# Sorting pass of a two-layer graph kernel: GpSimd is paced by later TensorE groups, and in the middle of each group too

## The chip, the cores and the metric

One Trainium2 chip, and one core of it. The metric is the device time of one execution in microseconds (us), the median over several.

## The reference, cut to what matters

Two graph layers over 6250 nodes and 206250 edges. For this change only the first matters, and of it the part before the sum over the edges of a source node:

```python
h = jnp.maximum(_layernorm(x, axis=-1), 0.0)
att_scores = jax.nn.sigmoid(head_rel @ att_w + att_b)      # head = h[src], rel by edge type
neighbor_emb = att_scores * tail                           # tail = h[dst], 64 wide
aggr_emb = jax.ops.segment_sum(neighbor_emb, edge_index[0], num_segments=N_ENTITIES)
```

The second layer sums over the same source nodes (`segment_sum(msg_j, row, ...)`). The edges come ordered by `dst`, and both sums go by `src`. So the kernel first sorts the edges by `src`: it writes one record per edge to HBM at the place that it has in the order of `src`. A record is `REC` = 100 numbers: the edge's 32 attributes, its two nodes, its gate, a pad, and its 64 gated values.

## The kernel before

The kernel runs as one stage after another: `front`, `sort` (the sorting pass, 220 to 2870 us of the trace), `relation_layer`, `relation_nodes`, and the second layer. The change lies in `sort` alone.

**Tiles, groups, chunks.** `P` = 128 edges, one per partition, are a tile. `G` = 4 tiles are a group. A chunk is `T` = 26 tiles, so `GROUPS` = 7 groups, of which the last has two tiles. There are `CHUNKS` = 62 chunks, 434 groups. A loop turn (`Fori` over `i`) has two chunks, `n = 2*i` and `2*i + 1`, with double buffers `b`. The turns `i = 0` and `i = 30` are written out, the others are a loop.

**Engines.** Every engine has its own program, and semaphores that count groups tie them together. A program is worked through in its order.

- TensorE, per group q: three "rows" matmuls (3 partitions by 512 columns) that spread the low digit, the source and the destination of each edge over all partitions: `p_lo` (L666), `p_src` (L668), `p_dst` (L670). `p_dst` raises `s_dst`. Then `p_place` (L674), four matmuls. Then `look` for the group before, q-1: twelve matmuls `p_look` (L643), the last of which raises `s_look`, and twelve matmuls `p_h` (L653), which raise `s_h`. These 28 load 128x128 weights each. `p_src` of a group waits for VectorE's ranks of the group before (`s_ranked`).
- VectorE, per group q: `table_rest` (L847), `dst_hot` (L850, waits for `s_dst` of q and `s_h` of q-2), `table_low` (L852), `same_before` (L860, four of them, ends with `s_ranked`), then `picked` of group q-1 (L807, waits for its `s_look`), the one-hot tiles of the next chunk (L511, L512), a sum (L815) and `logit` (L820). `place` (L826) comes once a chunk, after its last group.
- ScalarE, per group: `table` (L708), `lo_away` (L711), `lo_hot_t` (L714), the gate (L724), `h_gated` (L730). Once a chunk it assembles the records in `rec[b]` and raises `s_ready`.
- SyncE: per chunk the loads `fields`, `window`, `stage`, and a write of zeros to `q_starts`.
- GpSimd: 26 indirect DMAs per chunk (L625, "scatters"), one per tile, that write `rec[b][:, t, :]` to `records` at `place[b][:, t]`.

**What paces GpSimd.** A chunk's scatters may begin when its places and records are there (`s_place`, `s_ready`; ScalarE has them in group 2 of the chunk after). From `i = 1` on, GpSimd also waits for `s_dst` at t = 4, 8, 12, 16, 20, 24: at tile t of chunk n, until `p_dst` has been done for `7*n + LEAD + t/4` groups in all, with `LEAD` = 12. `rows_spread` gives this number. In the written-out last turn (chunks 60 and 61) it is cut off at 434. Tiles t = 0 to 3 have no such wait, so the scatters t = 24, 25 and 0 to 3 of the next chunk go under one wait. After each wait GpSimd raises a semaphore `s_passed`, which nothing waits for.

**Buffers.** `rec[b]` and `place[b]` are written again for chunk n+2, when all 26 scatters of chunk n have landed (`s_sent[b]`).

Of the kernel before, what the change touches and what calls it, by code (L numbers as in the profile page):

```python
# [36 lines left out]
G = 4  # L37
# [23 lines left out]
LO, NODE, TO = 0, 1, 2  # L61
H3 = 2 * D + D // 2
STEP_A, STEP_B, STEP_C, STEP_D = 7, 10, 13, 23
LEAD = 12
COLS = -(-NT // P)
LAST_COLS = NT - (COLS - 1) * P

# [32 lines left out]
def loop(eng, body):  # L100


    body(0)
    with eng.Fori(1, PAIRS - 1) as i:
        body(i)
    body(PAIRS - 1)
# [45 lines left out]
def at_start(i, b=0):  # L152
    return isinstance(i, int) and i == 0 and b == 0
# [361 lines left out]
def sort(k):  # L515
# [5 lines left out]
    with ExitStack() as ctx:  # L521
# [49 lines left out]
        def rows_spread(n, g):  # L571

            ahead = n * GROUPS + LEAD + g
            return min(ahead, CHUNKS * GROUPS) if isinstance(n, int) else ahead
# [9 lines left out]
        with nc.Block() as block:  # L584
            @block.sync
            def _(sp):
                sp.wait_ge(s_set, 2)

                def body(i):
                    for b in range(2):  # L590
                        n = 2 * i + b
                        wait(sp, s_dst, (n - 1) * GROUPS)
                        sp.dma_start(fields[b][:], k.field_rows[:, bass.ds(n * P * T, P * T)]).then_inc(s_fields[b], 16)
                        base = sp.value_load(k.base_i[0:1, bass.ds(n, 1)], min_val=0, max_val=ROWS - P)
                        wait(sp, s_h, (n - 1) * GROUPS)
                        sp.dma_start(window[b][:], k.h3_table[bass.ds(base, P), :]).then_inc(s_window[b], 16)
                        if not at_end(i, b):
                            wait(sp, s_staged, n - 1)
                            sp.dma_start(stage[b][:], attr_v[bass.ds(n, 1), :, :, :].rearrange("c p t e -> (c p) t e")).then_inc(s_attr[b], 16)

                        sp.dma_start(q_starts_v[:, bass.ds(n * T, T), :], zero_q[:].rearrange("p (t c) -> p t c", c=QW)).then_inc(s_zq, 16)

                loop(sp, body)
                sp.wait_ge(s_zq, 16 * CHUNKS)
                for b in range(2):
                    sp.wait_ge(s_sent[b], SCATTERED * PAIRS)

            @block.gpsimd
            def _(pool):
                def body(i):  # L610
                    for b in range(2):
                        n = 2 * i + b
                        if not at_start(i, b):
                            pool.wait_ge(s_place, n + GROUPS)
                            pool.wait_ge(s_ready, n + GROUPS)
                            pool.sem_inc(k.s_passed, 1)
                        for t in range(T):
                            if at_start(i, b) and t % G == 0:
                                pool.wait_ge(s_place, t // G + 1)
                                pool.wait_ge(s_ready, t // G + 1)  # L620
                                pool.sem_inc(k.s_passed, 1)
                            elif not (isinstance(i, int) and i == 0) and t > 0 and t % G == 0:
                                pool.wait_ge(s_dst, rows_spread(n, t // G))
                                pool.sem_inc(k.s_passed, 1)
                            nc.gpsimd.indirect_dma_start(  # L625
                                k.records, bass.IndirectOffsetOnAxis(ap=place[b][:, t:t + 1], axis=0),
                                rec[b][:, t, :], None).then_inc(s_sent[b], 16)

                loop(pool, body)
# [1361 lines left out]
```

## Time and profile before

| | |
|---|---|
| median of 3 runs | 5864.14 us (5855.48 to 5867.09) |
| the profiled execution's own time | 5865.56 us |
| its span, first to last instruction | 5863.7 us |
| sorting pass, from the first scatter to the last | 233.4 to 2866.3 us |
| mean granted TensorE clock over the span | 0.531 |

The span is what the trace covers, and 1.9 us lie around it. Engines in the rows: PE is TensorE, PEld its weight loads, DVE VectorE, ACT ScalarE, POOL GpSimd, SPq SyncE's DMA queue. A row of the timeline is the start, the duration, the engine, the line, the operation and its tiles, and in brackets how long the engine had been idle before it and what released it. "remote" and "issue" as releasers mean that the profile could not put the end of the wait down to a recorded instruction. Ends of matmuls are modelled: a PE row says when a matmul was issued, not when its result was there. When it was there is seen in the engine that waited for it.

### The profile page before, as it was taken

How to read it: one execution, taken by the hardware profiler on the slowest of the kernel's cores; microseconds unless marked ns; L12 is line 12 of the kernel's file. 1: busy time of each engine (PE TensorE's matmuls, PEld its weight loads, DVE VectorE, ACT ScalarE, POOL GpSimd, SP SyncE). 2: the span in 40 equal slices, each digit the busy share in tenths (PEclk: the TensorE clock that was granted, in tenths of full speed). 3: DMA queues.
4: the chain of work that ended last, by engine and by line, in shares of the span. 5: the costliest groups of instructions: out<-in, count | busy, mean ns of one | idle time of the engine just before them, and what ended most of it. 6: DMA issues, size and time to landing. Idle time of an engine off the chain costs nothing. (4 is left out here: it accounts for less than half of the span.)

```text
span 5863.7 us, 79660 instructions
## 1 busy us (share of the span) xinstructions
PE 2726.4 (46%) x21110; PEld 1693.1 (29%) x21111; DVE 3881.4 (66%) x8751; ACT 2758.0 (47%) x5413; POOL 3278.9 (56%) x3388
## 2 busy tenths in 40 slices
PE   7655555555555555555488622322223222222223
PEld 7433333333333333333388511111111111111102
DVE  9867777777777777776599645655556666655552
ACT  3244444444444444444122345655555555555552
POOL 0146565666666565656610266666666666666653
PEclk8555555555555555555577755555555555555555
DMA  5112121212121212121477533433334343433321
GB/s 64 55 54 71 63 71 62 71 63 71 63 71 63 71 63 71 63 71 58 103 160 145 72 103 100 124 110 108 108 103 111 109 110 103 110 108 109 109 79 24
DMA packets 691304, 505.28 MB, mean 86 GB/s; under 512 B 588446, under 2 KB 605214, under 8 KB 691109
## 3 DMA queue, kind: packets, MB, share of 16 engines
q1 hardware_dynamic: 573012, 246.99, 18.2%
q0 software_dynamic: 108736, 196.93, 11.6%
q10 hardware_dynamic: 9360, 59.56, 2.7%
q14 instruction: 172, 1.40, 0.1%
q8 instruction: 24, 0.39, 0.0%
HBM read 289.96 MB, written 213.26 MB: 86 GB/s over the span
## 5 line engine op out<-in xcount | busy, mean ns | idle before, releaser
L625 POOL DMA_INDIRECT records<-rec,place x1612 | 1557.2, 966 | 1306.9 <-issue 451.0
L1395 POOL DMA_INDIRECT got_a<-kv_table,idx_a x1612 | 1539.5, 955 | 762.8 <-issue 691.9
L860 DVE SCALAR_TENSOR_TENSOR same_before<-p_src,src_f,before 128x128 bf16<-128x128 f32 x1612 | 775.0, 535 | 0.0
L711 ACT ACTIVATE lo_away<-p_lo,minus_number 128x512 bf16<-128x512 f32 x434 | 291.2, 671 | 615.5 <-remote 593.6
L668 PE MATMUL p_src<-fields,select 3*128 3x512 bf16 x434 | 248.3, 572 | 687.7 <-DVE same_before L860 512.0
L1411 PE MATMUL p_a<-ident,flat_attr 128*128 128x128 f32 x434 | 123.5, 433 | 930.5 <-issue 447.4
L807 DVE TENSOR_TENSOR picked<-p_look,hi_hot 128x392 f32<-128x392 f32 x434 | 231.5, 533 | 407.5 <-remote 398.2
L1420 PE MATMUL p_a<-relu,w_t 128*128 128x512 f32 x248 | 230.8, 1034 | 463.4 <-issue 332.5
L850 DVE TENSOR_SCALAR dst_hot<-p_dst,number 128x512 bf16<-128x512 f32 x434 | 307.3, 708 | 191.1 <-remote 178.1
L643 PE MATMUL p_look<-table_low,lo_hot_t 128*128 128x98 bf16 x1612 | 410.2, 281 | 0.0
L643 PE MATMUL p_look<-table_rest,lo_hot_t 128*128 128x98 bf16 x1612 | 409.4, 280 | 0.0
L1545 DVE TENSOR_TENSOR prod<-got_a,wide 128x1664 f32<-128x1664 f32 x62 | 117.0, 1888 | 440.2 <-remote 216.3
L643 PE MATMUL p_look<-table,lo_hot_t 128*128 128x98 bf16 x1612 | 402.3, 278 | 0.0
L730 ACT ACTIVATE h_gated<-p_h,gate_s 128x64 f32<-128x64 f32 x1586 | 372.1, 315 | 51.5 <-remote 12.2
L653 PE MATMUL p_h<-window,dst_hot 128*128 128x64 bf16 x4836 | 357.6, 242 | 65.1 <-issue 64.9
L1014 PE MATMUL acc<-high,lo_r 128*128 128x64 bf16 x1708 | 345.4, 244 | 60.0 <-DVE low L1079 40.7
L708 ACT COPY table<-p_place 128x49 f32<-128x49 f32 x434 | 91.7, 211 | 597.0 <-issue 371.6
L1411 PEld LDWEIGHTS p_a<-ident,flat_attr 128*128 128x128 f32 x434 | 75.6, 215 | 978.3 <-issue 824.4
L1014 PE MATMUL acc<-rest_r,lo_r 128*128 128x64 bf16 x1708 | 344.3, 243 | 0.0
L1014 PE MATMUL acc<-low,lo_r 128*128 128x64 bf16 x1708 | 344.2, 243 | 0.0
L653 PEld LDWEIGHTS p_h<-window,dst_hot 128*128 128x128 bf16 x4836 | 312.2, 133 | 54.2 <-issue 53.8
L1014 PEld LDWEIGHTS acc<-high,lo_r 128*128 128x128 bf16 x1708 | 291.3, 171 | 67.6 <-issue 66.3
(377 smaller groups left out, 8443.3 us busy)
## 6 DMA issues: line engine op xcount, KB each, us to landing
sums<-packed_a ACTq DMA_DIRECT2D x62, 936.0 KB
q_starts<-zero_q SPq DMA_DIRECT2D x62, 884.0 KB
rec_r<-records SPq DMA_DIRECT2D x124, 442.0 KB
qin<-q_starts SPq DMA_DIRECT2D x62, 884.0 KB
attr_a<-records SPq DMA_DIRECT2D x62, 442.0 KB
records<-rec,place POOLq DMA_INDIRECT x1612
got_a<-kv_table,idx_a POOLq DMA_INDIRECT x1612
stage<-in_edge_attr SPq DMA_DIRECT2D x61, 416.0 KB
```

What stands on the lines that cost most here:

```text
L625: nc.gpsimd.indirect_dma_start(k.records, bass.IndirectOffsetOnAxis(ap=place[b][:, t:t + 1], axis=0), rec[b][:, t, :], None).then_inc(s_se ...
L643: last = nc.tensor.matmul(p_look[qb][:, j * 2 * HI:(j + 1) * 2 * HI], lo_hot_t[qb][:, j * P:(j + 1) * P], part, start=(e == 0), stop=(e == 2))
L653: last = nc.tensor.matmul(p_h[qb][:, j * D:(j + 1) * D], dst_hot[qb][:, j * P:(j + 1) * P], part, start=(e == 0), stop=(e == 2))
L668: nc.tensor.matmul(p_src[:, 0:m * P], k.select[:, NODE, :], rows, start=True, stop=True).then_inc(s_src, 1)
L711: nc.scalar.activation(lo_away[qb][:, 0:m * P], p_lo[:, 0:m * P], ACT.Abs, bias=k.minus_number[:]).then_inc(s_lo_away, 1)
L730: last = nc.scalar.activation(to, p_h[qb][:, j * D:(j + 1) * D], ACT.Copy, scale=gate[b][:, t:t + 1])
L807: v.tensor_tensor(picked[:, 0:n, :, :], p_look[gb][:, 0:n * 2 * HI].rearrange("p (g a h) -> p g a h", a=2, h=HI), bc(group_hot(k, b, g, HI ...
L850: v.tensor_scalar(dst_hot[qb][:, 0:m * P], p_dst[:, 0:m * P], k.number[:], None, ALU.is_equal).then_inc(s_dst_hot, 1)
L860: last = v.scalar_tensor_tensor(same_before[:, first:first + j + 1, :].rearrange("p g e -> p (g e)"), p_src[:, 0:(j + 1) * P], k.src_f[:, ...
L1014: last = nc.tensor.matmul(acc[:, to(t // SUPER)], lo[b][:, :, t], part, start=False, stop=True, skip_group_check=True)
L1395: nc.gpsimd.indirect_dma_start(got[b][:, t, :], None, k.kv_table, bass.IndirectOffsetOnAxis(ap=idx[b][:, t:t + 1], axis=0)).then_inc(s_got ...
L1420: nc.tensor.matmul(p_a[:, 0:c1 - c0], k.w2_t[:], relu[:, c0:c1], start=True, stop=True).then_inc(s_net, 1)
```

## The change

Two edits. `LEAD` goes from 12 to 14, so each wait at t = 4, 8, ... is for two groups more of `p_dst`. And a second kind of wait is added in the middle of each group of scatters, at t = 2, 6, 10, 14, 18, 22: until `look` has been done for `7*n + 13 + (t-2)/4` groups (`rows_spread(...) - 1`). Both hold in all turns but the first.

```diff
-LEAD = 12
+LEAD = 14
...
                             elif not (isinstance(i, int) and i == 0) and t > 0 and t % G == 0:
                                 pool.wait_ge(s_dst, rows_spread(n, t // G))
                                 pool.sem_inc(k.s_passed, 1)
+                            elif not (isinstance(i, int) and i == 0) and t % G == G // 2:
+                                pool.wait_ge(s_look, rows_spread(n, t // G) - 1)
+                                pool.sem_inc(k.s_passed, 1)
                             nc.gpsimd.indirect_dma_start(
                                 k.records, bass.IndirectOffsetOnAxis(ap=place[b][:, t:t + 1], axis=0),
                                 rec[b][:, t, :], None).then_inc(s_sent[b], 16)
```

## Rows read from the trace of the kernel before

**Rows 1.** The page: the span, and its costliest group, with its idle time.

```profile
span 5863.7 us, 79660 instructions
...
L625 POOL DMA_INDIRECT records<-rec,place x1612 | 1557.2, 966 | 1306.9 <-issue 451.0
```

**Rows 2.** Busy time by stretch: us, then each engine's busy us (x instructions), clock, DMA share.

```profile
276.80:310.50 33.70, 25.38 (x227) 14.85 (x225) 32.71 (x123) 21.07 (x64) 0.38 (x1) 0.50 0.05 16
...
321.80:348.40 26.60, 1.63 (x3) 0.23 (x3) 2.69 (x10) 2.30 (x7) 17.24 (x18) 0.50 0.11 37
...
1498.40:1539.60 41.20, 23.23 (x204) 13.62 (x203) 29.57 (x109) 19.56 (x60) 25.21 (x26) 0.50 0.23 78
...
1622.00:1664.80 42.80, 23.39 (x205) 13.48 (x203) 30.23 (x111) 19.74 (x60) 24.98 (x27) 0.50 0.18 55
```

**Rows 3.** Who waited for whom, 500 to 2500 us: in total, times, longest.

```profile
DVE picked L807 <- remote: 283.3, 95, 6.1
DVE dst_hot L850 <- remote: 135.7, 40, 4.9
DVE table_rest L847 <- issue: 72.8, 24, 3.3
...
POOL records L625 <- issue: 343.6, 1059, 2.1
POOL records L625 <- PE p_dst L670: 225.0, 107, 2.5
POOL records L625 <- remote: 222.7, 85, 3.2
```

**Rows 4.** Timeline of POOL: the scatter after each longer pause, and two others.

```profile
1505.62 0.96 POOL L625 DMA_INDIRECT records<-rec,place  x1 [2.33 <-PE p_dst L670]
1506.88 0.96 POOL L625 DMA_INDIRECT records<-rec,place  x1 [0.30 <-issue]
...
1512.25 0.96 POOL L625 DMA_INDIRECT records<-rec,place  x1 [1.88 <-PE p_dst L670]
...
1524.58 0.96 POOL L625 DMA_INDIRECT records<-rec,place  x1 [2.52 <-remote]
...
1529.77 0.96 POOL L625 DMA_INDIRECT records<-rec,place  x1 [0.30 <-issue]
...
1537.11 0.96 POOL L625 DMA_INDIRECT records<-rec,place  x1 [2.59 <-remote]
...
1546.83 0.96 POOL L625 DMA_INDIRECT records<-rec,place  x1 [2.42 <-PE p_dst L670]
```

**Rows 5.** Timeline of all engines in the run of scatters from 1524.58 us.

```profile
1523.80 0.75 DVE L850 TENSOR_SCALAR dst_hot<-p_dst,number 128x512 bf16<-128x512 f32 x1 [4.84 <-remote]
...
1526.47 0.56 DVE L807 TENSOR_TENSOR picked<-p_look,hi_hot 128x392 f32<-128x392 f32 x1
...
1527.01 0.63 PE L670 MATMUL p_dst<-fields,select 3*128 3x512 bf16 x1
...
1528.43 0.74 DVE L850 TENSOR_SCALAR dst_hot<-p_dst,number 128x512 bf16<-128x512 f32 x1
...
1528.64 0.28 PE L643 MATMUL p_look<-table_low,lo_hot_t 128*128 128x98 bf16 x1
...
1534.65 0.57 DVE L807 TENSOR_TENSOR picked<-p_look,hi_hot 128x392 f32<-128x392 f32 x1 [3.47 <-remote]
```

**Rows 6.** Timeline: VectorE's wait at the end of the next run, of six scatters.

```profile
1545.82 0.57 DVE L807 TENSOR_TENSOR picked<-p_look,hi_hot 128x392 f32<-128x392 f32 x1 [1.83 <-remote]
```

**Rows 7.** Timeline of DVE and POOL: before chunk 1's scatters, and around them.

```profile
281.28 0.74 DVE L850 TENSOR_SCALAR dst_hot<-p_dst,number 128x512 bf16<-128x512 f32 x1
...
311.63 0.96 POOL L625 DMA_INDIRECT records<-rec,place  x1 [34.45 <-ACTq L762]
...
343.25 0.96 POOL L625 DMA_INDIRECT records<-rec,place  x1 [0.30 <-issue]
...
348.40 0.57 DVE L807 TENSOR_TENSOR picked<-p_look,hi_hot 128x392 f32<-128x392 f32 x1 [23.92 <-remote]
```

**Rows 8.** Timeline of DVE, POOL and ACT at the end of the pass.

```profile
2799.39 0.96 POOL L625 DMA_INDIRECT records<-rec,place  x1 [6.74 <-PE p_dst L670]
...
2802.86 0.48 DVE L850 TENSOR_SCALAR dst_hot<-p_dst,number 128x256 bf16<-128x256 f32 x1
...
2825.07 0.36 DVE L807 TENSOR_TENSOR picked<-p_look,hi_hot 128x196 f32<-128x196 f32 x1 [14.94 <-remote]
...
2830.75 0.52 ACT L730 ACTIVATE h_gated<-p_h,gate_s 128x64 f32<-128x64 f32 x2 [4.49 <-remote]
...
2834.66 0.96 POOL L625 DMA_INDIRECT records<-rec,place  x1 [7.43 <-issue]
...
2866.31 0.96 POOL L625 DMA_INDIRECT records<-rec,place  x1 [0.30 <-issue]
...
2871.83 5.99 SPq L964 DMA_DIRECT2D rec_r<-records  x4
```

## The prediction, made before the change was run

> **What bounds the kernel now.** I read the page first, then the busy time by stretch, the waits, and last the timeline, because the pass repeats itself from chunk to chunk and one turn tells nearly all.
>
> The page says that the scatters are the costliest group of the kernel, 1612 of 0.966 us, and that GpSimd stands idle before them for 1306.9 us in all [rows 1]. So GpSimd isn't simply full. By stretch, a chunk takes 41.20 us, and one in four takes 42.80, 1.6 more. VectorE is busy for 29.57 to 30.23 us of that, GpSimd for 25.21, TensorE for 23.23 by its modelled rows, ScalarE for 19.56, and the DMA engines to 23% [rows 2]. No engine is full. The mean chunk is (3 x 41.20 + 42.80) / 4 = 41.6 us.
>
> While GpSimd had nothing to do (276.8 to 310.5 us) VectorE was busy for 32.71 of 33.70 us [rows 2]: without scatters the pass is bound by VectorE. In the steady stretch VectorE loses 283.3 + 135.7 + 72.8 = 492 us of 2000 to long waits, before `picked`, `dst_hot` and `table_rest` [rows 3]. That is 492 x 41.6 / 2000 = 10.2 us a chunk, and it is what separates 41.6 from some 31.
>
> Whom it waits for is seen in the timeline. `picked` at 1534.65 needs `look` of the group before, whose last matmul was issued at 1528.64, 6.0 us earlier; `dst_hot` at 1528.43 got its `p_dst` within 1.4 us of its issue at 1527.01 [rows 5]. So results of TensorE come promptly for a while and then hardly at all. The limit is in the scatters. Without waits, 26 of them ran from 311.63 to 344.2, one every 1.265 us, and VectorE stood for 23.92 us before `picked`, until 348.40, 4.2 us behind the last of them [rows 7]; TensorE issued 3 matmuls in those 26.6 us [rows 2]. At the end of the pass the last `look` reached VectorE 14.94 us late, again while scatters ran [rows 8]. I call that starvation: in a long run of scatters TensorE's 128-row matmuls stop finishing. What in the chip does it the trace doesn't say.
>
> The waits on `s_dst` cut the runs. Pauses come before 1505.62, 1512.25, 1524.58, 1537.11 and 1546.83 [rows 4], at t = 4, 8, 16, 24 and 4 again, so the runs have 4, 8, 8 and 6 scatters, and take 6.63, 12.33, 12.53 and 9.72 us: 1.66, 1.54, 1.57 and 1.62 us a scatter. Over the bare 1.265 that is 1.57, 2.21, 2.41 and 2.13 us a run; 26 x 1.265 + 8.32 = 41.2 us. So the chunk is GpSimd's time: 32.9 us of scatters and 8.3 us of pauses in which TensorE catches up. Within a run about the first three scatters cost TensorE nothing (the prompt `dst_hot` above stands 3.85 us behind the restart), then it starves to the run's end: `look` is there 0.13 us behind the run of eight that ends at 1534.52 [rows 5], and 1.42 us behind the run of six that ends at 1544.40 [rows 6].
>
> **What the change does, part by part.**
>
> 1. More instructions on GpSimd: six waits a chunk, each with an increment. The wait of before at t = 20, which was already satisfied, shows 0.30 us before its scatter (1529.77), the same as a scatter without a wait (1506.88) [rows 4]. So a satisfied wait costs 0, hidden behind the scatter before it. If that cover were gone it would cost at most what a real restart does, 0.78 us (below) less 0.30, 2.9 us a chunk. I take 0, by the nearer row.
>
> 2. `LEAD` 14 alone shifts GpSimd two groups later against TensorE. The records of a chunk are then there three groups before their first scatter instead of one, and the last scatter of chunk n goes some 2 groups, 12 us, before `place` of chunk n+2 needs it landed. Nothing new is late. Steady cost 0. What is queued behind each wait is only GpSimd's own scatters.
>
> 3. The waits on `look`. These change where a run can stop. Before, a run that starves TensorE stopped at `p_dst`; then TensorE had to finish `look`, `p_h` and three rows matmuls before the next scatter, `dst` being 1.68 us behind `look` (1536.33, the restart at 1537.11 less the 0.78 us that lie between `dst_hot` at 1523.80 and the restart at 1524.58). Now it can stop at `look`, and restart 0.78 us behind it, with `p_h` and rows done in the new run's free first scatters. A run of eight that stops at `look` takes 8 x 1.265 - 0.30 + 0.13 + 0.78 = 10.7 us by the one row and, with the 1.42 us of the other, 12.0 (1.34 to 1.50 a scatter). A run of six takes 6 x 1.265 - 0.30 + 1.42 + 0.78 = 9.5 us (1.58). How long are the runs? After a restart at `p_dst`, `look` must be there within 3.0 us (it was, 2.67 us behind, at 1526.47), the next `p_dst` within 5.5 (it was, 4.63 behind), the next `look` within 8.1 (it wasn't: 10.85). So that run stops after six. After a restart at `look`, the next that starves is `p_dst` after six (about 1.53 a scatter, with 1.1 us for rows) or `look` after eight. I take the mix at 1.54 a scatter: 26 x 1.54 = 40.0 us, and 0.4 us for the longer pause in one chunk of four. 40.4 against 41.6 is -1.2 us a chunk. With chunks 3 to 59 that is 57 x -1.2 = -68 us.
>
> 4. The ends. At the start, chunk 2 gets its third scatter about two groups later, while TensorE runs unhindered: 0. At the end of the pass the waits are cut off at 434. Before, chunk 60 had 22 scatters left at 2799.39, 434 groups of `p_dst` were there by 2802.86, and chunk 61 began at 2834.66, held by ScalarE's `h_gated` at 2830.75, itself starved [rows 8]. Now chunk 60 has 24 scatters left when `look` 433 comes, about 1.3 us behind `p_dst` 434: 2804.1 + 0.78 + 24 x 1.265 = 2835.2. Chunk 61 follows at once if TensorE's last 24 matmuls (12 `p_h`, 6 `look`, 6 `p_h`) fit in the free first scatters (+0.5 us), or comes as before 7.5 us behind the run's end (+8). I take +4. The next stage starts 5.5 us behind the last scatter, as now [rows 8].
>
> Sum: -68 + 4 = -64 us against the profiled execution's 5865.56, which is 1.4 above the median: 5800 us.
>
> A rule speaks against any of this. The Trainium skill, page "SBUF — State Buffer", section "SBUF: two separate sides", has only GpSimd and VectorE share an engine port, and TensorE wait for no one. By that rule the scatters cannot starve TensorE; VectorE's instructions would be what they lengthen. The rows show the reverse: TensorE's results were late by 23.92 us beside scatters, and VectorE's `dst_hot` takes 0.74 us beside them (1528.43) as without (281.28) [rows 5, 7]. By the rule the sum is 0 for part 3; by the rows it is -68.
>
> **Rivals.**
>
> - *More stops, same pause each.* If a pause of some 2 us at `look` doesn't let TensorE recover (`p_h` and rows are still undone), runs shrink to four. The run of four cost 1.66 a scatter, more than any other [rows 4]: 26 x 1.66 + 0.4 = 43.5 us, +1.9 x 57 + 4 = +112, 5976 us. It decides once the mean passes 1.585 a scatter (41.2 us). For it: cost a scatter falls with the length of the run in four of four. Against it: that pause was spent before `p_dst`, with TensorE's whole backlog in it. Chance 0.29.
> - *Conserved.* TensorE is always either working or starved, and its 23.2 us of work plus what 26 scatters take from it (41.6 - 23.2 = 18.4, 0.71 us each) doesn't depend on their order. Then nothing moves but the end: 5864 + 4 = 5868. For it: three shapes of run lie within 8% a scatter. Against it: the first scatters of a run cost nothing and those in the long run 1.2 us each [rows 7]. The skill's rule ends here too. Chance 0.13.
> - *Starvation ends.* If stops after two or four scatters keep TensorE in the free part always, GpSimd itself is the floor, 26 x 1.265 = 32.9 us, or 34 with some pauses: -7.6 x 57 = -433, about 5435 us. For it: VectorE needs only 30. Against it: GpSimd needs 4.70 us a group of 4.62, so it has no time for pauses in which nothing is late. Chance 0.07.
>
> **How the numbers follow.** My forecast, 1.44 to 1.57 a scatter, has 0.51: 5650 to 5850 us. With the last rival, faster has 0.58; same (within 0.2%, 12 us, about what a measurement of this kernel can tell from no change) 0.13; slower 0.29. The likeliest is 5800 us. The range leaves out the last rival and the worst of the first: 5640 to 5965 us.
>
> **What would show it.** In the changed kernel's timeline: pauses before scatters at t = 2, 6, ... with `look` as the last to come; runs of six or eight; `picked`'s waits near 0 to 2 us and less than 8.5 us a chunk in all; GpSimd's restart 0.78 us behind `picked`. Runs of four with pauses of 1.5 us or more at each stop would make the prediction wrong, and so would a scatter that costs TensorE the same wherever it stands in a run. The clock stays at 0.50 in the pass either way, and stages behind 2870 us only shift.

## The result, and the profile after

The changed kernel took 5922.33 us (median of 4 executions, 5908.23 to 5942.2) against 5863.1 us before (5855.48 to 5867.09): ratio 1.0105, with a 95% interval of 1.0086 to 1.0124. It is slower by 1.05%, where I had forecast 5800 us, 1.1% faster. The profiled execution took 5931.75 us, with a span of 5929.9.

The groups of one line, with first and last start, show where. (A row of this kind has the shortest, middle and longest duration in ns, then the first and last start in us.) The scatters (L628 now, L625 before) and the first of the three matmuls of `add` in the relation layer (L1017 now, L1014 before), in the changed kernel:

```profile
L628 POOL DMA_INDIRECT records<-rec,place x1612: 952/958/1192, 232.7 to 2867.8; - x180
```

```profile
L1017 PE MATMUL acc<-high,lo_r x1708: 210/251/275, 2886.6 to 3341.6; 128*128 128x64 bf16 x190
```

and the same matmuls of the kernel before:

```profile
L1014 PE MATMUL acc<-high,lo_r x1708: 225/251/273, 2885.0 to 3288.8; 128*128 128x64 bf16 x190
```

The pass went from 2632.9 us [rows 1 give its count, rows 8 its last scatter, at 2866.31] to 2635.1: +2.2, nothing in sum. The relation layer, in which no line was changed, went from 403.8 to 455.0 us: +51. The rest of the 66 us between the two profiled executions lies in the attention layer. Its gathers (L1398 now, L1395 before) span 2290 us before and 2303 after, but 2284 in another profiled execution of the same changed kernel (experiment 2). So these 13 us come and go with the same program, and I don't count them for the change.

The 2.2 us hide three shifts. Counted in the timelines, 26 scatters to a chunk:

| us | first scatter to chunk 3 | chunks 3 to 59 | chunks 60 and 61 |
|---|---|---|---|
| before | 182.8 | 2371.7 | 78.4 |
| changed | 190.1 | 2378.3 | 66.8 |
| moved | +7.3 | +6.6 | -11.6 |
| forecast | 0 | -68 | +4 |

**The pass.** The groups of 500 to 2500 us in the changed kernel; its idle time counts 0.30 us before each scatter:

```profile
L628 POOL DMA_INDIRECT records<-rec,place x1245 | 1206.9, 969 | 794.5 <-remote 338.7 <-issue 331.1 <-PE p_dst L673 66.7
```

```profile
L853 DVE TENSOR_SCALAR dst_hot<-p_dst,number 128x512 bf16<-128x512 f32 (+1 forms) x335 | 237.0, 708 | 247.7 <-remote 247.6
L810 DVE TENSOR_TENSOR picked<-p_look,hi_hot 128x392 f32<-128x392 f32 (+1 forms) x336 | 179.1, 533 | 194.1 <-remote 190.1 <-issue 4.0
```

1245 scatters in 2000 us are 26 x 2000 / 1245 = 41.8 us a chunk; before, 791.3 us of idle time and 1251 scatters [rows 3 by releaser] make 41.6. The stops add up to 794.5 - 1245 x 0.30 = 421 us, 8.8 a chunk, against 416 and 8.6. In sum they hardly changed; they moved: VectorE waits 190 us for `look` where it waited 283, and 248 for `dst_hot` where it waited 136 [rows 3].

The stops do stand where the forecast put them, in the timeline of GpSimd (those over 1 us, 1500 to 1560 us):

```profile
1504.06 0.96 POOL L628 DMA_INDIRECT records<-rec,place  x1 [2.02 <-remote]
...
1513.73 0.96 POOL L628 DMA_INDIRECT records<-rec,place  x1 [2.40 <-remote]
...
1523.22 0.96 POOL L628 DMA_INDIRECT records<-rec,place  x1 [1.99 <-remote]
...
1532.64 0.96 POOL L628 DMA_INDIRECT records<-rec,place  x1 [2.01 <-remote]
...
1542.20 0.96 POOL L628 DMA_INDIRECT records<-rec,place  x1 [2.29 <-remote]
...
1554.82 0.95 POOL L628 DMA_INDIRECT records<-rec,place  x1 [2.70 <-PE p_look L646]
```

Four runs of six scatters take 9.67, 9.49, 9.42 and 9.56 us, one of eight 12.62: 1.59 us a scatter for the sixes, 1.58 for the eight. Over chunks 4 to 59 there are 248 stops over 1 us: 122 at the new waits, 112 at the old ones, and 14 at t = 9, where no wait stands (2.05 us, in one chunk of four, in the kernel before too). Between them lie 165 runs of six at 1.60 us a scatter, 34 of eight at 1.57 and 18 of four at 1.63.

**The relation layer.** Its start, busy time in steps of 10 us (PE, PEld, DVE, ACT, POOL, clock, DMA share, GB/s). The changed kernel:

```profile
2880.00:2890.00 10.00, 3.09 (x41) 2.89 (x41) 9.40 (x7) 3.16 (x2) 8.17 (x7) 0.50 1.07 227
2890.00:2900.00 10.00, 4.36 (x33) 3.32 (x33) 2.07 (x2) 0.00 (x0) 7.87 (x8) 0.50 0.75 168
2900.00:2910.00 10.00, 2.29 (x14) 1.62 (x15) 0.00 (x0) 0.00 (x0) 7.56 (x9) 0.50 0.30 83
...
2920.00:2930.00 10.00, 0.64 (x3) 0.57 (x4) 0.00 (x0) 0.00 (x0) 7.56 (x9) 0.50 0.29 83
...
2950.00:2960.00 10.00, 8.64 (x127) 8.53 (x128) 9.57 (x8) 3.16 (x2) 0.00 (x0) 0.50 0.89 175
```

and the kernel before:

```profile
2880.00:2890.00 10.00, 5.00 (x75) 5.01 (x76) 9.78 (x7) 2.15 (x2) 8.35 (x6) 0.50 0.93 202
2890.00:2900.00 10.00, 8.39 (x124) 8.16 (x123) 9.56 (x8) 3.16 (x2) 8.48 (x6) 0.67 1.07 224
...
2920.00:2930.00 10.00, 8.12 (x120) 7.89 (x119) 9.44 (x8) 3.16 (x2) 8.48 (x6) 0.83 0.93 198
```

At the layer's start GpSimd issues its 48 gathers of `second` at once, and SyncE loads the records chunk by chunk. Before, the loads keep the DMA engines at 0.8 to 1.07 of their time, a gather takes GpSimd 1635 ns in the mean, and TensorE issues some 120 matmuls in 10 us. After, TensorE falls to 3 or 4 matmuls in 10 us while gathers follow each other. It waits for no signal that the profile shows, and the data of both chunks that it worked on had been there since VectorE's last `low`, at 2892.1:

```profile
2922.28 0.21 PE L1017 MATMUL acc<-rest_r,lo_r 128*128 128x64 bf16 x1 [2.59 <-issue]
2925.09 0.21 PE L1017 MATMUL acc<-low,lo_r 128*128 128x64 bf16 x1 [2.60 <-issue]
2927.88 0.21 PE L1017 MATMUL acc<-high,lo_r 128*128 128x64 bf16 x1 [2.58 <-issue]
```

VectorE then waits 52 us:

```profile
2944.14 0.20 DVE L1072 TENSOR_TENSOR rel<-rec_r,base 128x26 bf16<-128x26 f32 x1 [52.04 <-remote]
```

The row says "remote", but the loads of the first four chunks had landed by 2900 (from 2905 to 2943 the DMA view has GpSimd's gathers and two instruction packets alone), so what was missing is TensorE's signal for the first chunk. Its 78 matmuls are all issued by 2900.7 in TensorE's rows; that the signal came some 43 us later is seen at VectorE alone. Meanwhile VectorE makes no `rest`, so SyncE loads no records. The gathers took 1.5 to 1.8 us beside the loads and 0.95 without them (1032 ns in the mean of the 48), and the hole ends at 2944, 6 us behind the last of them. It looks like what I had called starvation, in a stage that I had let "only shift".

### The profile page after: what moved, and what is told of

Read it like the earlier page. It is cut to its first block and busy times, and to the rows that moved or that the text cites. A ratio compares the mean times of both kernels' runs of the same rounds, so it can differ in the third digit from the quotient of the medians.

```text
span 5929.9 us, 80136 instructions
## 1 busy us (share of the span) xinstructions
PE 2754.0 (46%) x21110; PEld 1700.6 (29%) x21111; DVE 3878.3 (65%) x8751; ACT 2765.7 (47%) x5413; POOL 3260.7 (55%) x3388
## 5 line engine op out<-in xcount | busy, mean ns | idle before, releaser
L628 POOL DMA_INDIRECT records<-rec,place x1612 | 1561.9, 969 | 1303.7 <-issue 433.1
L1398 POOL DMA_INDIRECT got_a<-kv_table,idx_a x1612 | 1546.2, 959 | 769.2 <-issue 610.5
L656 PE MATMUL p_h<-window,dst_hot 128*128 128x64 bf16 x4836 | 379.1, 241 | 156.9 <-issue 156.8
L1017 PE MATMUL acc<-high,lo_r 128*128 128x64 bf16 x1708 | 346.5, 246 | 75.6 <-DVE low L1082 41.9
L1533 DVE TENSOR_TENSOR relu<-relu,soft 128x896 f32<-128x896 f32 x62 | 67.9, 1095 | 454.1 <-issue 293.2
L1017 PE MATMUL acc<-rest_r,lo_r 128*128 128x64 bf16 x1708 | 345.3, 245 | 15.6 <-issue 15.6
L1017 PE MATMUL acc<-low,lo_r 128*128 128x64 bf16 x1708 | 345.2, 245 | 13.1 <-issue 13.1
L1017 PEld LDWEIGHTS acc<-high,lo_r 128*128 128x128 bf16 x1708 | 290.2, 170 | 83.5 <-issue 82.7
```

The source lines that it names most:

```text
L628: nc.gpsimd.indirect_dma_start(k.records, bass.IndirectOffsetOnAxis(ap=place[b][:, t:t + 1], axis=0), rec[b][:, t, :], None).then_inc(s_se ...
L656: last = nc.tensor.matmul(p_h[qb][:, j * D:(j + 1) * D], dst_hot[qb][:, j * P:(j + 1) * P], part, start=(e == 0), stop=(e == 2))
L1017: last = nc.tensor.matmul(acc[:, to(t // SUPER)], lo[b][:, :, t], part, start=False, stop=True, skip_group_check=True)
L1398: nc.gpsimd.indirect_dma_start(got[b][:, t, :], None, k.kv_table, bass.IndirectOffsetOnAxis(ap=idx[b][:, t:t + 1], axis=0)).then_inc(s_got ...
```

## The experiments

Two conditions have to be told apart to read them. The runs were made in batches, and every batch also timed the kernel before, on the same chip. In 6 of the 11 batches it took 5025 to 5028 us (each batch's median), in the other 5, as on record, 5863 to 5874. One chip showed both, in different batches. Within a batch there was never a mixture of the two. I call them the free and the stalling condition. A kernel's times are compared only within its batch; rows of profiles, one execution each, are compared across batches of one condition. I could not choose the condition, and the trace doesn't show what sets it.

The expectations count the stages whole. In them the pass is some 20 us longer than from first to last scatter (2653 for the 2633 above), and the relation layer 16 us longer than its `acc` matmuls (420 for 404, 471 for 455).

**1. The parts alone, and the gathers paced, in the free condition.** Four kernels, one batch: `LEAD = 14` alone; the waits on `s_look` alone, with `LEAD = 12`; and the changed kernel and the kernel before, each with this in the relation layer:

```diff
                 for h in range(SECOND):
+                    pool.wait_ge(s_used, h + 1)
+                    pool.sem_inc(k.s_passed, 1)
                     nc.gpsimd.indirect_dma_start(
                         second[:, h, :], None, by_pair,
```

> The kernel before with LEAD = 14 and no waits at the lookup. The changed kernel lost 51.3 us in the relation layer (471 us against 419.5), where no line was changed, 13.4 us in the attention layer and 2.2 us in the pass. Theory A (the pass is conserved whatever the waits, and the relation layer tips between two ways of running by a small shift of its start): the pass stays within 5 us of 2653 us, and the total is either near 5863 (layer at 420) or near 5920 (layer at 470), with nothing between. Theory B (the lookup waits alone are to blame for all of it): 5863 within 10 us, layer at 420. My guess between the two levels: 5863.

> The changed kernel with LEAD = 12 and the waits at the lookup kept (now 11 groups ahead). Theory A: the pass within 5 us of 2653 us and the relation layer at 420 or at 470, so a total near 5863 or near 5920. Theory B: near 5920, with the layer at 470. Against both, my forecast for the stops at the lookup (1.54 us a scatter in place of 1.60) would have the pass at about 2585 us here.

> The changed kernel with one thing more: in the relation layer GpSimd issues its 48 gathers of second one for each chunk that TensorE has added (it waits for s_used to reach 1, 2, ... 48) in place of all at once at the start. Theory A (TensorE is held up by GpSimd's gathers issued back to back, one every 1.03 us from 2891 to 2938 us, and the 52 us hole is that): the hole is gone, the relation layer takes 400 to 425 us and the total 5855 to 5880. Rival C (the hole has to do with TensorE's clock or with where its program is loaded, not with the gathers): the layer stays near 470 us and the total near 5922.

> The kernel before with the same pacing of the 48 gathers of second. Theory A: the layer ran at 419.5 us without a hole, with the gathers slowed to 1.6 us each by the loads of records; spread out they cost the loads less, so 400 to 420 us and a total of 5843 to 5863. Rival C: no change, 5863 within 6 us. If the pacing itself harms (a gather that waits is late for the last eight additions), over 5870.

The kernel before took 5027.61 us. LEAD alone: 5036.5, ratio 1.0018 (1.0009 to 1.0027). The waits alone: 5028.67, 1.0003 (0.9994 to 1.0012). The changed kernel paced: 5036.69, 1.0016 (1.0007 to 1.0025). The kernel before paced: 5027.18, 0.9999 (0.999 to 1.0008). None of the expectations could be tried, because the level was another. The fourth kernel's pass is that of before, and shows the free condition, from its page and in the stretch that stood for the starvation in [rows 2]:

```profile
L625 POOL DMA_INDIRECT records<-rec,place x1612 | 1553.0, 963 | 750.6 <-issue 469.6
```

```profile
321.80:348.40 26.60, 17.72 (x156) 10.32 (x157) 22.39 (x84) 15.59 (x47) 18.71 (x20) 0.50 0.28 92
```

The same program, GpSimd at 20 scatters in 26.6 us (18 there), and TensorE issues 156 matmuls where it issued 3. There is no stop in the steady part, a chunk is 26 x 1.265 = 32.9 us, and the scatters end at 2305.9. What LEAD costs here is one stop, before the third chunk's fifth scatter, first with LEAD alone, then as before:

```profile
341.48 0.96 POOL L625 DMA_INDIRECT records<-rec,place  x1 [9.96 <-PE p_dst L670]
...
349.18 0.95 POOL L625 DMA_INDIRECT records<-rec,place  x1 [2.97 <-PE p_dst L670]
```

```profile
333.26 0.96 POOL L625 DMA_INDIRECT records<-rec,place  x1 [2.20 <-PE p_dst L670]
```

With GpSimd as the bound a stop isn't regained: these stops are 12.3 us against 1.9 (and 0.8 in the next chunk), and the time is 9 us longer. The first three kernels were run again to meet the stalling condition, together and one by one, and met the free one:

> LEAD = 14 alone once more, for a chip on which the kernel before takes 5863 us. On the chip of the first four (kernel before 5027.6 us) it lost 9 us, in the first stop of GpSimd. Runs of the changed kernel on the slower chip fell into two heaps, 5859 to 5877 (4 runs) and 5904 to 5942 (10 runs), 45 us apart, as the hole in the relation layer is or isn't there; the kernel before has 5846 to 5885. Theory A (the hole tips by chance, at a rate that hangs on how the pass ends): LEAD = 14 alone keeps the runs of scatters long at the end of the pass and stays in the lower heap, 5860 to 5880. Theory F (LEAD = 14 brings the hole): over half of the runs above 5895.

> The waits at the lookup with LEAD = 12 once more. Theory A: the stops at the lookup bring TensorE nearer to GpSimd at the end of the pass and with it the hole: over half of the runs above 5895, the rest near 5860. Theory F: nearly all runs 5850 to 5875. The pass itself: 2645 to 2660 us if the time of a chunk is conserved, about 2585 by my forecast.

> The changed kernel with its 48 gathers of second spread over the first 48 chunks of the relation layer, once more. Theory A: no run has the hole; all runs 5850 to 5875 (the changed kernel less the 51 us), relation layer 420 us. Rival C: the heap above 5900 stays.

> The waits at the lookup alone (LEAD = 12), for a chip on which the kernel before takes 5863 us. There the changed kernel's runs lie near 5860 without the hole in the relation layer and near 5905 with it. If these waits bring the hole, most runs are above 5895 and the layer takes 470 us in the trace; if LEAD = 14 brings it, nearly all are 5850 to 5880 with a layer of 420 us. The pass: 2650 to 2660 us if the time of a chunk is conserved, 2585 us by my forecast. On a chip on which the kernel before takes 5025 us: 5027 to 5029 as twice before.

> LEAD = 14 alone, for a chip on which the kernel before takes 5863 us. The pass keeps its 2653 us within 5 (the 10 us longer first stop, seen on the faster chips, is given back, as in the changed kernel). If LEAD = 14 brings the hole in the relation layer, over half of the runs are above 5895 and the layer takes 470 us; if the waits at the lookup bring it, the runs are 5850 to 5880 and the layer takes 420 us. On a chip on which the kernel before takes 5025 us: 5033 to 5037 as twice before.

LEAD alone took 5035.06 against 5024.68 us, and 5034.59 against 5025.81; the waits alone 5027.42 against 5024.68, and 5028.45 against 5027.01; the changed kernel paced 5033.42 against 5024.68.

**2. The changed kernel again.**

> The changed kernel itself once more. In the first four experiments the kernel before took 5027.6 us on another chip than in the runs on record (5863), with a pass of 2093 us in place of 2653: there GpSimd issued its scatters at 1.27 us each all through, without a pause, and TensorE kept up. Theory D (the starvation of TensorE belongs to the chip the kernel runs on): where the kernel before takes 5027, the changed kernel takes 5036 to 5039 (10 us from the longer first stop of GpSimd, seen with LEAD = 14 alone), with a relation layer of 420 us; where the kernel before takes 5863, it takes 5908 to 5942, with a hole in the relation layer. Rival E (the state changes from run to run on one chip): a mixture of both levels among the runs of one chip.

The stalling condition: 5904.79 us (ten executions) against 5863.02 (thirteen), ratio 1.0047 (1.0018 to 1.0076). The ten fall into two heaps: 5859, 5862, 5866, 5877, and six of 5904 to 5923. The profiled one is of the upper heap (5907.77) and has the hole; its scatters run from 233.2 to 2866.5, its `acc` matmuls from 2885.1 to 3340.2. So the change costs some 45 us in an execution of the upper heap and nothing measurable in one of the lower. That the lower heap has no hole is inferred: no such execution of this kernel was profiled. Theory D, that a chip has its condition, wasn't contradicted here and fell later, when a chip of the free condition came back in the stalling one.

This execution also shows that the hole doesn't hang on when the layer starts. Its first gather stands at 2872.74 (2872.57 before), its first `acc` matmul at 2885.1 (2885.0), and its first twelve gathers take what they take in the kernel before, within 0.03 us each. Yet from 2888.7 on TensorE loses time, and the kernel before doesn't.

**3. The gathers paced, in the stalling condition.** The third kernel of experiment 1.

> The changed kernel with its 48 gathers of second spread over the first 48 chunks of the relation layer, again, since the two calls before fell on chips on which the kernel before takes 5025 us and shows neither stops nor a hole. Where the kernel before takes 5863 us: Theory A (the hole is TensorE held up by the gathers issued back to back): no run has the hole, all runs 5850 to 5877, relation layer 420 us. Rival C (the hole doesn't hang on the gathers): the heap at 5904 to 5942 stays with over half of the runs, layer 470 us. Where the kernel before takes 5025 us: 5033 to 5037 as before, nothing learned.

5875.51 us (twelve executions, 5860.19 to 5903.02) against 5872.25; ratio 1.0016 (0.9998 to 1.0033). The profiled one:

```profile
L1019 PE MATMUL acc<-high,lo_r x1708: 225/253/273, 2889.9 to 3293.2; 128*128 128x64 bf16 x190
```

403.3 us, no hole, with the pass unchanged (scatters from 233.9 to 2871.6). This execution took 5862.08 us, one of the fastest of the twelve, so it alone proves little; the heaps say more. Two executions of twelve stand above 5900, at 5901 and 5903, where ten of fourteen without the pacing stand at 5904 to 5942. So rival C (over half above 5904) fell. Theory A came true in the main, but its "all 5850 to 5877" did not: six of twelve are above 5877, and what these have isn't known.

**4. Scatters farther apart, and the gathers in the middle of the layer.** First in the pass, with the gathers paced, in the free condition; then with them back to back behind 20 chunks, in the stalling one.

```diff
                                 rec[b][:, t, :], None).then_inc(s_sent[b], 16)
+                            if not (isinstance(n, int) and n == 0 and t == 0):
+                                pool.wait_ge(s_filler, n * T + t)
+                                pool.sem_inc(k.s_passed, 1)
+                            nc.gpsimd.iota(filler[:], [[1, 128]], base=0, channel_multiplier=0).then_inc(s_filler, 1)
...
+                pool.wait_ge(s_used, 20)
+                pool.sem_inc(k.s_passed, 1)
                 for h in range(SECOND):
```

> The kernel before with the gathers of second paced and, in the pass, a small operation of GpSimd (an iota of 128 elements, about 0.23 us) behind every scatter, so that scatters start 1.50 to 1.55 us apart and not 1.27. If TensorE is starved by how densely the scatters follow each other, it keeps up at this rate: no stop of GpSimd is left, a chunk takes 26 x 1.53 = 39.8 us (41.2 before), and the pass 2560 to 2600 us, the total about 5780. If it is starved by every long run of scatters, however spaced, the stops stay and the filler comes on top: a chunk of 43 to 46 us, total 5950 to 6100. On a chip without the starvation, where a chunk is 32.9 us, the total would grow by 60 x 6.9 = 410 us to 5440.

> The kernel before with two edits in two stages, read apart in the trace, for a chip on which the kernel before takes 5863 us. In the pass: a small operation of GpSimd behind every scatter, which on a chip without the stops made a chunk 37 us in place of 33 (1.42 us a scatter). If TensorE is starved by how densely the scatters follow each other, it keeps up: no stops, a chunk of 37 to 38 us and the pass 2360 to 2420 us in place of 2653. If it is starved by every long run of scatters however spaced, the stops stay, a chunk takes 42 to 46 us and the pass 2650 to 2850. In the relation layer: the 48 gathers of second back to back as before, but only once TensorE has added 20 chunks. If back-to-back gathers starve TensorE whenever they come, a hole of 45 to 55 us lies there, in the middle of the layer (layer 470 us); if what counts is how the layer starts, there is none (420 us). On a chip on which the kernel before takes 5025 us: pass 2357, layer 420 us.

Free: 5290.99 us against 5024.68, ratio 1.0528 (1.0514 to 1.0542); a scatter starts every 1.42 us, not the 1.53 expected, a chunk is 36.9 us and one in four 38.7. Stalling: 6005.44 against 5869.06, ratio 1.0235 (1.0203 to 1.0267). There, 500 to 2500 us:

```profile
L627 POOL DMA_INDIRECT records<-rec,place x1180 | 1162.7, 985 | 518.9 <-PE p_dst L676 198.8 <-issue 128.7 <-remote 123.7
```

44.1 us a chunk, of the 42 to 46 that the second theory had. Spaced out by 12%, the scatters still stall TensorE, if less: GpSimd stops for 44.1 - 37.4 = 6.7 us a chunk beyond its own work, where before it stopped for 41.6 - 33.0 = 8.6. The spacing costs 4.4 us a chunk and gives back 1.9. And in the layer there was no hole:

```profile
L984 POOL DMA_INDIRECT second<-records,idx x48 | 83.2, 1734 | 155.1 <-PE acc L1022 140.8 <-issue 14.3
```

48 gathers in a row, 1734 ns each, beside loads that are in full flow: TensorE wasn't held up. So gathers back to back are not enough for a hole. Whether it needs the layer's start isn't shown: this is one execution, and the kernel before, whose gathers do come at the start, had none in its profile either.

**5. The waits at the lookup alone, in the stalling condition** (second kernel of experiment 1).

> The waits at the lookup alone (LEAD = 12), again, for a chip on which the kernel before takes 5863 us. If these waits bring the hole in the relation layer, most runs are above 5895 and the layer takes 470 us in the trace; if LEAD = 14 brings it, nearly all are 5850 to 5880 with a layer of 420 us. The pass: 2650 to 2660 us if the time of a chunk is conserved, 2585 us by my forecast. On a chip on which the kernel before takes 5025 us: 5027 to 5029 as before.

5815.86 us (six executions, 5808.14 to 5825.86) against 5874.24 (eleven, 5854.35 to 5927.23): ratio 0.9867 (0.9816 to 0.9918). It is **faster** than the kernel before by 1.3%, where the changed kernel was slower in its two batches. The expectation had over half above 5895 if these waits brought the hole: none is. The kernel before showed two heaps here, six of 5854 to 5874 and five of 5909 to 5927; against the lower heap alone (mean 5865) the gain is 0.8%. The scatters, whole and from 500 to 2500 us:

```profile
L628 POOL DMA_INDIRECT records<-rec,place x1612: 956/962/1212, 233.0 to 2832.4; - x180
```

```profile
L628 POOL DMA_INDIRECT records<-rec,place x1261 | 1218.4, 966 | 782.5 <-remote 362.2 <-issue 301.6 <-PE p_look L646 74.7
```

The pass is 2599.4 us, 33.5 less than before, with 41.2 us a chunk and 8.3 of stops in it. That is between the expectation's "conserved" and my forecast, 2619 as it counts, against 2650 to 2660 and 2585. Of the 33.5 us, 4.6 lie ahead of chunk 3, 21.7 in chunks 3 to 59 and 7.2 behind. The runs are more mixed: 113 of six at 1.57 us a scatter and 34 of eight at 1.53, but also 47 of four and 31 of two, at 1.62 and 1.86. The `acc` matmuls take 403.7 us, no hole. The profiled execution is 49 us shorter than that of the kernel before; the other 14 us lie in the attention layer (its gathers span 2276 us), where no line was changed, so the waits themselves may be worth nearer to 0.6% than to 0.8.

**6. A shorter LEAD.** The changed kernel with `LEAD = 10` and the gathers paced.

> The changed kernel with LEAD = 10 in place of 14 and the gathers of second paced through the relation layer: the version that the experiments point to for the condition in which the kernel before takes 5870 us. There the waits at the lookup with LEAD = 12 took 5816, with a pass of 2619 against 2653 and 2655 us before and after. Theory G (each two groups of LEAD cost GpSimd time at every stop, because it waits for a signal that TensorE gives later): LEAD = 10 takes 5750 to 5800, with a pass of 2560 to 2600. Theory H (12 is the turning point: with less distance GpSimd runs up to the rows' own dependence and the stops come at the chunks' starts): a pass of 2640 us or more, 5830 to 5900. The pacing takes the upper heap of runs (45 us more) away in both. In the other condition: 5010 to 5025, the first stop shorter by up to 10 us than with LEAD = 12.

That was the free condition: 5024.48 us against 5027.41, 0.9993 (0.9983 to 1.0002). Again:

> The waits at the lookup with LEAD = 10 and the gathers of second paced, again, for the condition in which the kernel before takes 5870 us. Theory G (each two groups of LEAD cost time at every stop): 5750 to 5800, with a pass of 2560 to 2600. Theory H (12 is the turning point): a pass of 2640 us or more, 5830 to 5900. In between: a pass near the 2619 us of LEAD = 12, less at most the 10 us of a shorter first stop, 5795 to 5820. In the other condition 5024 as before.

Stalling: 6115.16 us against 5870.59, ratio 1.0423 (1.0408 to 1.0437). GpSimd's stops over 1 us at 1560 to 1615 us, and the group from 500 to 2500:

```profile
1567.69 0.96 POOL L628 DMA_INDIRECT records<-rec,place  x1 [6.25 <-issue]
...
1579.95 0.95 POOL L628 DMA_INDIRECT records<-rec,place  x1 [2.47 <-remote]
1582.96 0.95 POOL L628 DMA_INDIRECT records<-rec,place  x1 [2.06 <-issue]
...
1593.88 0.96 POOL L628 DMA_INDIRECT records<-rec,place  x1 [2.39 <-remote]
...
1606.23 0.96 POOL L628 DMA_INDIRECT records<-rec,place  x1 [2.56 <-remote]
...
1614.69 0.96 POOL L628 DMA_INDIRECT records<-rec,place  x1 [6.25 <-issue]
```

```profile
L628 POOL DMA_INDIRECT records<-rec,place x1125 | 1079.9, 960 | 924.4 <-issue 599.7 <-remote 319.8 <-PE p_look L646 4.9
```

46.2 us a chunk. GpSimd now gets so near that it stands some 6 to 8 us at each chunk's first scatter (56 of 56 chunks), where the only waits are those for the chunk's places and records, on top of its paced stops. Theory G fell, and H's mechanism held, though its 5830 to 5900 us was too low by 215: 12 is the best of the three distances.

**7. LEAD = 14 alone, for the stalling condition**, was tried twice more, and never met it:

> LEAD = 14 alone. Where the kernel before takes 5870 us: by Theory G it lies above the kernel before by what the changed kernel lies above the waits alone, 35 us of pass: pass 2670 to 2700 us, runs at 5885 to 5905 and, with the hole, at 5930 to 5950. By rival J (14 and 12 are alike without the waits at the lookup, and only the pair of edits is bad): pass 2650 to 2660. In the other condition 5035 as three times before.

> LEAD = 14 alone, for the condition in which the kernel before takes 5870 us. With the waits at the lookup, a chunk of the pass took 46.2 us at LEAD = 10, 41.0 at 12 and 41.75 at 14; without them 41.6 at 12. If LEAD = 14 costs by itself, what it adds to the waits (10 us in the first stop and 0.75 us a chunk), the pass takes 2675 to 2700 us here. If it costs only the first stop, and a chunk is 41.6 us whatever the distance: 2655 to 2670. If it costs nothing here (rival J): 2650 to 2655. The hole of 45 to 50 us in the relation layer comes or not, run by run, in all three. In the other condition 5035 as four times before.

5036.21 us against 5027.41, 1.0016 (1.0007 to 1.0025), and 5034.78 against 5025.53, 1.0018 (1.0009 to 1.0027): the free condition's value. Whether 14 costs the pass something without the waits at the lookup stays open.

## Why the prediction was wrong

The forecast was -64 us, all in the pass; the profiled executions differ by +66. Of these 130 us, 66 lie in the pass, 51 in the relation layer and 13 in the attention layer, which come and go. Two steps failed.

**"Stages behind 2870 us only shift": this step failed, and it made the result slower.** The relation layer took 51 us more. The prediction had found that scatters starve TensorE and didn't look for the next place where GpSimd issues indirect DMAs in a row, 5 us behind the pass. With the gathers paced the profiled execution had no hole and the changed kernel's 1.0105 and 1.0047 became 1.0016 (0.9998 to 1.0033): not measurably slower, and not faster either. The hole isn't made by the change alone: the kernel before has an upper heap too, in 6 of 61 executions (the 4 on record and those of the stalling batches), the changed kernel in 10 of 14, the waits alone in none of 6. What makes it so much likelier with both edits stays open.

**Part 3, the mix at 1.54 a scatter: too low, the term was mis-sized.** The waits alone gave (41.2 - 0.4) / 26 = 1.57, not 1.54: -22 us in the 57 chunks, not -68. With `LEAD` 14, as changed, it was (41.8 - 0.4) / 26 = 1.59, and +7. The mechanism came true in part: stops at `look` exist, and runs are of six and eight. But the run of eight, which had to bring the gain at 1.34 to 1.50, cost 1.57, and the run of six that ends at `p_dst`, taken at 1.53, cost 1.61 (88 of them, 9.64 us each). The stop before a six or an eight is 2.0 to 2.8 us whatever signal ends it, so restarting at `look` saves little.

**Part 2, LEAD steady cost 0: wrong in this kernel.** With the same waits, 14 in place of 12 made the pass 35.7 us longer (2635.1 against 2599.4, one profiled execution each, in different batches), of which 28 us in chunks 3 to 59. The two other profiled executions with 14 and these waits (experiments 2 and 3) have 2374 and 2381 us there, against 2350 with 12. It took back what part 3 won. Why the stops add up to more with 14 isn't known. Part 4's "0" at the start was wrong too, by 7.3 us. The changed kernel's first long stop there,

```profile
384.89 0.96 POOL L628 DMA_INDIRECT records<-rec,place  x1 [12.44 <-PE p_look L646]
```

was 5.82 us before. In the free condition the like cost 9 us of the kernel's time. The end was better than the +4, at -11.6: chunk 61 followed at once, so the 7.43 us of [rows 8] are gone.

**Part 1, satisfied waits at 0: right.** In the free condition nearly all are satisfied, and the six more a chunk cost 0.03% (-0.06 to 0.12%).

**The rivals.** For the pass, *Conserved* came nearest: forecast 0 and the end, measured +2.2, with stops of 8.6 and 8.8 us a chunk before and after. That is luck in part: the end it had at +4 was -11.6, and the start paid it back. It isn't a law either: LEAD = 10 has 13.6 us of stops, the waits alone 8.3. *Starvation ends* never came by a kernel's doing; it came with the condition. *More stops* fell: runs stayed at six, not four. It had the side that was measured, slower, at a chance of 0.29, but by another cause. The rule of the Trainium skill that was weighed (page "SBUF — State Buffer", section "SBUF: two separate sides": TensorE waits for no one) fits the free condition, where 26 scatters and more in a row cost TensorE nothing that shows. In the stalling one TensorE does stand beside them, but no run shows that it stands for a port, so the rule is neither confirmed nor refuted there. That `dst_hot` takes 0.74 us beside scatters and without them shows that this one instruction isn't lengthened, and no more. The rows of one execution didn't show a property of the kernel, but of the kernel in a condition.

**What stays untested.** TensorE might stand for its own instructions, and not for anything that GpSimd holds. One row speaks against it in the pass: from 320 to 350 us, when it issued 3 matmuls in 26.6 us and then recovered, the DMA view of the kernel before has no instruction packet. In the relation layer an instruction packet falls at the hole's start in experiment 2's execution (2888 to 2890 us), but one falls there in the kernel before too.

## What to carry to other kernels

Where one engine's long runs of DMA issues hold another up, list every stage that has such a run, also behind the change, and spread those that have slack: one gather a chunk cost nothing that was measured in the free condition (0.9999), and with it the layer took 403.3 us in the stalling one, where it had taken 455.0. Before a pacing distance is tuned, try its two neighbours with the new waits: 10, 12 and 14 gave 46.2, 41.2 and 41.8 us a chunk. And time the kernel before beside every run: two levels 17% apart, and two heaps 0.8 to 1% apart within one of them, are each as large as what a pacing edit does, or larger.

## What the runs showed of the hardware

- The same program took 5025 or 5863 us, by the batch, on one chip too. In the free condition 20 scatters in 26.6 us leave TensorE 156 matmuls, in the stalling one 18 scatters leave it 3. The granted clock was 0.50 in both stretches. What sets the condition is open.
- In the stalling condition TensorE stood at 3 to 14 matmuls in 10 us beside indirect DMAs of 0.95 us back to back; beside such DMAs at 1734 ns each, slowed by loads, it didn't (one execution). A filler that spaced scatters from 1.27 to 1.42 us took the stops from 8.6 to 6.7 us a chunk.
- While TensorE stands, its matmuls come at multiples of 0.70 us: in the hole, from 2906 to 2944 us, each gap over 0.3 us is 0.7, 1.4, 2.1, 2.8 or 3.5 us within 0.03, and the same in experiment 2's hole. What beats at this step is open.
- An execution can fall into the hole or not with the same program: heaps of 5859 to 5877 and 5904 to 5923 us in one batch. Up to 3.6 us after the layer's first `acc` matmul, experiment 2's execution, with the hole, and that of the kernel before, without it, look alike there.
